# Zeroing the message table over eleven DMA engines in eight parts, and the first node rows ahead of the weights

## The reference

```python
h = jnp.maximum(_layernorm(x, axis=-1), 0.0)
z = jnp.concatenate([h[src], h[dst], edge_attr], axis=-1)            # 25000 x 160
m = sigmoid(z @ W_f + b_f) * softplus(z @ W_s + b_s)                 # 25000 x 64
message = jax.ops.segment_sum(m, src, num_segments=100000)
mean, var = message.mean(0), ((message - message.mean(0)) ** 2).mean(0)
out = x + h + (message - mean) * rsqrt(var + 1e-5) * gamma + beta
```

## Time and profile before

| | |
|---|---|
| median of 3 timed runs | 1071.09 us (1069.85 to 1071.23) |
| span of the profiled execution | 1087.2 us |
| POOL busy | 735.4 us (68%) |
| DVE busy | 742.1 us (68%) |
| PE busy | 579.7 us (53%) |
| ACT busy | 536.9 us (49%) |
| SP's queue (q1) | 111.46 MB, 29.0% of sixteen DMA engines' span |
| ACT's queue (q10) | 44.12 MB, 10.0% |
| POOL's queue (q0) | 20.09 MB, 16.5% |

### The profile page before, as it was taken

The page is one execution under the profiler, slowest core; times in us unless marked ns, Lnnn a source line. Parts: engine busy times, 40 slices in busy tenths (PEclk is TensorE's granted clock), DMA queues, the critical chain, the costliest instruction groups (busy, mean ns, idle before and its releaser), DMA issues. The chain is left out here.

```text
span 1087.2 us, 11011 instructions
## 1 busy us (share of the span) xinstructions
PE 579.7 (53%) x2442; PEld 406.6 (37%) x2442; DVE 742.1 (68%) x1551; ACT 536.9 (49%) x1185; POOL 735.4 (68%) x652
## 2 busy tenths in 40 slices
PE   0321754456553756664564556575636679844332
PEld 0121542335442534542352335454424479610000
DVE  3523766658766678757587666677566568789788
ACT  1131664556464656454565645664546556333332
POOL 7774777777878787777778777878787710650620
PEclk9855576765676565557666755655676579855555
DMA  7994443545443434434344334334333579589999
GB/s 280 416 402 151 111 124 75 123 94 123 104 120 77 125 59 79 85 56 83 62 83 78 86 53 86 62 78 82 63 76 58 153 290 410 195 254 414 416 404 387
DMA packets 88145, 176.02 MB, mean 162 GB/s; under 512 B 42561, under 2 KB 49285, under 8 KB 79663
## 3 DMA queue, kind: packets, MB, share of 16 engines
q1 hardware_dynamic: 34903, 111.46, 29.0%
q0 software_dynamic: 42880, 20.09, 16.5%
q10 hardware_dynamic: 10328, 44.12, 10.0%
HBM read 107.12 MB, written 68.50 MB: 162 GB/s over the span
## 5 line engine op out<-in xcount | busy, mean ns | idle before, releaser
L584 POOL DMA_INDIRECT m_buf<-in_x_dram,m_buf x384 | 368.4, 959 | 118.3 <-issue 111.6
L597 POOL DMA_INDIRECT msgs_dram<-sums,target x184 | 289.2, 1572 | 69.0 <-issue 56.0
L1164 PE MATMUL ps_all<-sums,m_last 128*128 128x64 f32 x920 | 152.2, 338 | 26.9 <-issue 23.7
L707 DVE TENSOR_REDUCE m_last<-late 128x24 f32<-128x1536 f32 (+1 forms) x49 | 85.3, 1741 | 113.8 <-ACT late L978 84.4
L1164 PEld LDWEIGHTS ps_all<-sums,m_last 128*128 128x128 f32 x920 | 145.9, 251 | 38.3 <-issue 35.4
L1117 PE MATMUL ps_all<-ident,m_last 128*128 128x128 f32 x49 | 21.2, 432 | 225.3 <-ACT sums L1036 212.0
L1138 PEld LDWEIGHTS ps_all<-m_buf 128*128 128x128 f32 x392 | 93.8, 328 | 50.0 <-issue 50.0
L1036 ACT ACTIVATE sums<-ps_all 128x256 f32<-128x256 f32 x46 | 17.6, 382 | 187.3 <-remote 187.3
L1027 ACT ACTIVATE m_last<-m_last,one_col 128x512 f32<-128x512 f32 x196 | 107.6, 550 | 1.6
L678 DVE SCALAR_TENSOR_TENSOR m_buf<-ps_all,m_buf 128x1024 f32<-128x1024 f32 x97 | 93.2, 960 | 19.3 <-remote 15.6
L827 DVE TENSOR_TENSOR y_kept<-ps_all,m_buf 128x256 f32 (+1 forms) x196 | 82.5, 422 | 26.6 <-remote 13.6
(11 more groups left out here) (171 smaller groups left out, 1076.1 us busy)
## 6 DMA issues: line engine op xcount, KB each, us to landing
m_buf<-msgs_dram SPq DMA_DIRECT2D x38, 1024.0 KB, 8.4
m_buf<-in_x_dram SPq DMA_DIRECT2D x48, 512.0 KB
out_dram<-m_buf ACTq DMA_DIRECT2D x20, 1024.0 KB, 10.8
msgs_dram<-y_kept SPq DMA_DIRECT2D x11, 1536.0 KB
m_buf<-src_rows_dram SPq DMA_DIRECT2D x47, 256.0 KB
y_spill_dram<-y_kept ACTq DMA_DIRECT2D x19, 512.0 KB
y_kept<-y_spill_dram SPq DMA_DIRECT2D x8, 1024.0 KB, 14.8
msgs_dram<-y_kept ACTq DMA_DIRECT2D x5, 1536.0 KB
```

The source lines that it names most:

```text
L584: pool.indirect_dma_start(xg[:, n % G_SLOTS, 2 * j + c, :], None, x, bass.IndirectOffsetOnAxis(ap=ids[:, c, n * TILES + j:n * TILES + j + ...
L597: pool.indirect_dma_start(msgs, bass.IndirectOffsetOnAxis(ap=target[:, n % UNROLL, j:j + 1], axis=0), comb[:, n % COMB_SLOTS, j, :], None, ...
L707: dve.tensor_reduce(row_ssq[:, rows], sq[:, rows, :], AX.X, ALU.add).then_inc(ssq_done, 1)
L1164: pe.matmul(ps_c[:, j, :], same_of(b, j, j + 1)[:, 0, :], msg_of(g)[:, b, :], start=(b == 0 and not begun), stop=(b == j), skip_group_chec ...
```

## The change

The zeroing of the 99968 rows that lie 781 to a partition is cut otherwise. The rows are seen as 11 stretches that follow one another in the table, each of 568 pieces of 16 rows (4096 B). Part k (of 8) writes 71 pieces of each stretch, all taken from one partition of `zeros`: stretch a from partition a. The leftover per partition is gone, since 11 x 568 x 16 is 99968. ACT issues parts 0 and 1 and no later ones; SP issues parts 2 and 3, 4 and 5, 6, and 7, each before (the last one after) the loads of groups 3, 4 and 5, and then the table's end. SP no longer waits for `zeros_set` itself. POOL waits for 9 DMAs instead of 18. And SP loads group 0's node rows and edge attributes before the weights.

```diff
-ZERO_PARTS = 16
-ZERO_EARLY = 5
+ZERO_WAYS = 11
+ZERO_PARTS = 8
 ZERO_FIRST = 2
+ZERO_AT = ((2, 4), (4, 6), (6, 7), (7, 8))
...
+    zero_rows = msgs[0:P * N_ROWS, :].rearrange("(a n r) f -> a n (r f)", a=ZERO_WAYS, r=BULK)
+
+    def zero_table(eng, k):
+
+        n = P * N_ROWS // (ZERO_WAYS * ZERO_PARTS * BULK)
+        eng.dma_start(zero_rows[:, k * n:(k + 1) * n, :],
+                      zeros[0:ZERO_WAYS, :].unsqueeze(1).to_broadcast([ZERO_WAYS, n, BULK * F])
+                      ).then_inc(table_zeroed, 16)
...
-        for u in range(SLOTS):
+        load(Group(0, 0))
+        load_weights()
+        for u in range(1, SLOTS):
             load(Group(0, u))
-        sp.wait_ge(zeros_set, 1)
-        done = ZERO_EARLY
         for u in range(SLOTS, UNROLL + 1):
-            end = min(ZERO_PARTS, 2 * ZERO_EARLY + 1 + 3 * (u - SLOTS))
-            for k in range(done, end):
-                zero_table(k)
-            done = end
+            for k in range(*ZERO_AT[u - SLOTS]):
+                zero_table(sp, k)
             if u < UNROLL:
                 load(Group(0, u))
+        over = (N_REST + DUMP) // FILL
+        sp.dma_start(msgs[P * N_ROWS:NODES + DUMP, :].rearrange("(p r) f -> p (r f)", p=FILL),
+                     zeros[0:FILL, 0:over * F]).then_inc(table_zeroed, 16)
...
             if n == ACC_FIRST:
-                pool.wait_ge(table_zeroed, 16 * (ZERO_PARTS + 2))
+                pool.wait_ge(table_zeroed, 16 * (ZERO_PARTS + 1))
...
-        for k in range(ZERO_FIRST, ZERO_EARLY):
-            zero_table(k)
```

More of the change, by code:

```diff
@@ L66 @@
 assert ALL_TILES == TILES * GROUPS and ITERS * UNROLL == LAST and UNROLL % SLOTS == 0 and UNROLL % G_SLOTS == 0
-assert UNROLL % S_SLOTS == 0
+assert UNROLL % S_SLOTS == 0 and P * N_ROWS % (ZERO_WAYS * ZERO_PARTS * BULK) == 0
 assert 0 < LAST_ROWS < BULK and (N_REST + DUMP) % FILL == 0 and LATE == 3
@@ L476, in sync, with load_weights @@
                          v[0:P - E_REST].rearrange("(p t) -> p t", t=1)).then_inc(ids_rest, 16)
[L478 to L486, removed]
+        def load_weights():
+            sp.wait_ge(w_cleared, 1)
+            for c, (w, b) in enumerate(((w_f, b_f), (w_s, b_s))):
+                cols = slice(c * F, (c + 1) * F)
+                sp.dma_start(w_z[0:F, cols], w[0:F, :]).then_inc(w_loaded, 16)
+                sp.dma_start(w_z[F:2 * F, cols], w[F:2 * F, :]).then_inc(w_loaded, 16)
+                for j in range(TILES):
+                    sp.dma_start(w_e[j * EF:(j + 1) * EF, j, cols], w[2 * F:2 * F + EF, :]).then_inc(w_loaded, 16)
+                sp.dma_start(b_row[:, cols], b.rearrange("(a f) -> a f", a=1).to_broadcast([SPLIT, F])
+                             ).then_inc(w_loaded, 16)
         def load_nodes(g):
@@ L947, in scalar @@
         act.wait_ge(zeros_set, 1)
[L948 to L952, removed]
         for k in range(ZERO_FIRST):
-            zero_table(k)
+            zero_table(act, k)
         act.preload_act_table_set("natural_log_exp_and_others")
```

## The result

| | before | after |
|---|---|---|
| median of the timed runs | 1070.49 us (1069.85 to 1071.23, 4 runs) | 1358.31 us (1357.26 to 1359.41, 4 runs) |
| span of the profiled execution | 1087.2 us | 1357.5 us |
| POOL busy | 735.4 us | 734.6 us |
| DVE busy | 742.1 us | 736.8 us |
| first accumulating scatter at | 106.54 us | 388.65 us |

The ratio is 1.2687, with a 95% interval from 1.2669 to 1.2705. The kernel became 27% slower, where 2% was forecast. The time is 13 us above the upper end of the range too. Of the cases that the prediction named, its first rival is the one that happened: the source of the zeros became the bound.

The account below looks back on a forecast made before the run. POOL's instruction list plus its wait for the zeroing bounds stage one. 4 + 89.8 + 20 + 3.8 + 8.4 = 126.0 put the first scatter at 127.8, +21.3 us profiled; 23 was taken for timed runs: 1094 us, range 1078 to 1345.

Parts of the forecast that it names:

- first rival: Zeroing's source: eleven engines reading partitions 0 to 10 share rates; 1339 us, chance 0.32 at about 1330; milder 1161, chance 0.05.
- What bounds the kernel: Stage one is POOL's instruction list plus one 13.0 us wait; a microsecond there is one at stage one's end.
- The rate: Zeroing: each DMA engine keeps about 25.9 GB/s, so eleven give 285 GB/s and the zeros take 89.8 us.
- The sum for eleven engines at full rate: Zeroing before POOL's first scatter: 4 + 89.8 + 20 + 3.8 + 8.4 = 126.0, first scatter at 127.8, +21.3 us.
- end piece: The 106-partition piece at the table's end, last in the zeroing on two engines: 8.4 us behind part 7.
- Are the eleven fed all the time?: Zeroing queues: the engines don't run dry while SP issues parts between loads, so no term was taken.
- POOL waits for nothing else: Stage one after the first scatter: POOL's next sums come in time, covered by 20 us and more.
- 2 or 3 us: ACT's issuing at 3.3 us: its second part may hold ACT this long, and nothing at the end waits.
- x of group 0 ahead of the weights: SP's first loads: DVE's 12.91 us wait shrinks to between 0 and about 5, worth nothing at the end.
- The two ends of POOL's wait before: Before POOL's first scatter: zeroing ends at 99.5, sums at 105.7; timed runs' first scatter between 100.3 and 106.5.
- Rival 2: Before POOL's first scatter: sums, not zeroing, stay last; the wait shrinks from 13 to perhaps 4 us, 1062; chance 0.05.
- Wrong if: the share is high while the GB/s are near 100: Sign in the DMA stretches that would refute the forecast: engines that wait for the source.

Follow-up runs that it names:

- experiment one: The changed kernel with the zeros read from partitions 0, 12, 24, ..., 120 instead of 0 to 10: 1095.06 us, ratio 1.0222.
- two: The changed kernel with the zeros read from partitions 0, 2, 4, ..., 20: 1173.75 us, ratio 1.0947.
- three: The changed kernel with the zeros read from partitions 0, 8, ..., 80: 1179.95 us, ratio 1.1016.
- experiment four: The kernel before with group 0's node rows and edge attributes loaded ahead of the weights, zeroing on sixteen engines: 1072.32 us, ratio 1.0004.
- experiment five: The kernel before with the table's end written over sixteen engines as 32 x 53 pieces of 256 B: 1066.81 us, ratio 0.9954.
- experiment six: The changed kernel with zeros from partitions 12 apart and the table's end over sixteen engines: 1089.13 us, ratio 1.0166.
- seven: The kernel before with group 0's rows loaded ahead of the weights and the table's end over sixteen engines: 1066.03 us, ratio 0.9953.
- eight: The changed kernel with the weights loaded ahead of group 0's node rows again: 1358.4 us, ratio 1.2683.

## Why the prediction was wrong

**What bounds the kernel.** Right. A microsecond more in POOL's wait was one at the end: from the first scatter to the end of the span it is 968.9 us in the changed kernel, and 967.6, 967.9, 967.0, 967.1 and 967.0 in experiments one to five, wherever the first scatter lay.

**The rate: the step that failed.** "An engine does not get faster when its neighbours are idle. Eleven engines are 285 GB/s." The first sentence holds: 24.0 GB/s of all traffic for one in experiment one. The second doesn't follow from it. Both rows it rests on read from many partitions: the earlier trace rows from 128, and the earlier trace rows with two engines from 106. The changed kernel reads from eleven, in three groups, and has 102 GB/s, of which the zeros are 73.5. The term in the sum that it set, 89.8 us for the zeros on each engine, became some 384 (from the first issue near 4 us to the first scatter at 388.65, with what else the engines did in it). The rival said "No row of the kernel before has several engines reading a few neighbouring partitions", and that the rows showed it neither way. The forecast then took the rate of the nearest row all the same. It was nearest in the number of engines, but the number of partitions read was what mattered. Rival 1 should have been the likeliest case, the more so as a rule of the Trainium skill spoke for it ("SBUF — State Buffer", "Door 1: The DMA port swizzle"). That section doesn't say whether its figures are of loads or of stores; experiments one to three show the sharing for reads from SBUF.

**Rival 1's size.** The mechanism was right, and the time, 1339, was 19 us short. Its end of the zeroing was too early by 13.7 us (first scatter near 375, measured 388.65): I had 12 us beside 4 + 359, and it took some 26. Most of the rest is the base. The forecast counted from the profiled 106.54, while 102.27 is where POOL's wait ends in experiment four; 388.65 - 102.27 = 286.4, and with the 1070.49 measured beside the changed kernel that gives 1356.9, 1.4 us under the 1358.31. What the 26 us consist of I can't say to the microsecond. The end piece on two engines is in it (4.6 us in experiment six), and so are the loads, gathers and spills. Splitting them was not tried.

**The sum for eleven engines at full rate.** Experiment one is the case that the sum describes:

| step | forecast | measured (experiment one) |
|---|---|---|
| first scatter | 127.8 | 124.90 |
| POOL's wait before it | 34 | 31.15 |
| shift of the time | +23 | +23.2 (1095.06 - 1071.9) |
| share and GB/s, 20 to 115 us | 0.75 to 0.8, about 300 | 0.81 and 311 (20 to 40) |
| end piece | 8.4 | 4.6 to 6.0 came back by spreading it |
| POOL's further waits in stage one | none | none beyond issue |

The rate of an engine held: SP's queue, which is mostly zeros, moved 17.70 MB from 20 to 80 us in the kernel before, at a share of 74.0%, and 12.62 MB at 52.9% in experiment one. Both are 24.9 GB/s for a busy engine (the 24.0 above are of all traffic, the gathers too). That the time came within 1 us is in part luck: the first scatter came 2.9 us before the sum's, the kernel before, going by experiment four, has its own some 4 us before the 106.54 that the sum starts from, and 23 us were chosen between 21 and 28.

**"Are the eleven fed all the time?"** Right in its conclusion, as far as the end goes: in experiment one the first scatter comes within 3 us of the sum, which has no term for it. In the changed kernel the premise was gone. Two parts held SP 23.19 us at 71 us, and the loads of groups 1 to 5 were issued from 56 to 287 us, since an engine moved a third of what it did before.

**POOL waits for nothing else.** Wrong: it waits 65.4 us for a centred buffer, at no cost to the end. The wait follows from the same cause, by a path that the prediction had at "2 or 3 us": ACT's two parts were issued in 0.97 us, but the two small stores behind them took 48 us to issue, and ACT went on at 124.57.

**x of group 0 ahead of the weights: worth nothing.** Right: experiments four, seven and eight, at three places of the first scatter. "DVE's first centring before 15 us" was right as well (8.96). "The weights start 0.8 us later" is right for the first (4.15 against 3.28 in the kernel before). The last of them was issued at 52 in the changed kernel, and that I had not foreseen.

**The two ends of POOL's wait before.** The prediction had "between 100.3 and 106.5" for the timed runs, with the remote waits perhaps gone. Experiment four has 102.27, with the zeroing last, and costs the same time as the kernel before, so this was right. That the sums come close behind the zeroing was not: in experiments four and five they are ready 28 and 21 us before the first scatter. Rival 2 (the sums stay last) had still less room than 0.05 gave it.

**"Wrong if: the share is high while the GB/s are near 100."** That is the row from 20 to 40 us, 0.74 and 102. This sign was named ahead, and it was the one that came.

## What to carry to other kernels

Before a DMA is forecast by the rate of its engines, count the partitions that it reads, and how many engines read from partitions that share a port: eleven neighbouring rows as a source gave 102 GB/s, and eleven rows 12 apart gave 311 GB/s with the same engines (all traffic from 20 to 40 us). Here a share that is high while the GB/s are low meant that the engines waited for the source. The two numbers alone don't say so; the experiment that moves only the source does. Where the rows nearest to a change differ from it in one respect, and a rival turns on that respect, the row isn't evidence for the forecast. And a tail on two of sixteen engines is worth looking for: spreading it gave 5 us, the only gain over the kernel before in this study.

## What the runs showed of the hardware

**SP's small loads slow down with the zeroing.** The same four loads of 8 KB each take SP the longer to issue, the slower the pieces in the queues go. In the order: experiment one, two and three (the changed kernel's are 16.23 us, above):

```profile
6.64 4.83 SPq L497 DMA_DIRECT2D m_buf<-in_L_gnn_W_f_dram  x4
```

```profile
5.84 9.00 SPq L497 DMA_DIRECT2D m_buf<-in_L_gnn_W_f_dram  x4
```

```profile
6.89 9.03 SPq L497 DMA_DIRECT2D m_buf<-in_L_gnn_W_f_dram  x4
```

1.2, 2.3, 2.3 and 4.1 us for one, or 1 to 1.9 to 1.9 to 3.4, go with the number of engines that share (one, two, two, up to four). The kernel before has 5.21 us for its first four, as in experiment one, and 1.98 us for the next four, from 12.93. Why SP's issue, on a queue of its own, depends on the transfers of ACT's queue was not tested.

**The profiled execution of the kernel before was not an ordinary one.** Its span is 16 us above its timed median, where every other kernel's is within 5 us of its own. 12 to 14 us of it lie behind the first scatter: 980.7 us to the end instead of 967.0 to 968.9. Of these, one wait of POOL in stage two shows most. Before:

```profile
POOL m_buf L1595 <- ACT late L1036: 48.1, 1, 48.1
```

And the same wait in experiment five:

```profile
POOL m_buf L1595 <- ACT late L1036: 33.1, 1, 33.1
```

Ahead of the first scatter it was slower too: group 0's sums are copied 31 us later than in experiments four and five (105.33 against 73.98 and 73.84). What held ACT in that execution the profile doesn't say ("remote" in the earlier trace rows), and it stays open. The forecast's care with this gap (23 us of shift instead of 21.3) was right.
